# A two-layer gated cross-attention kernel: second attention with values centred in advance, gates placed by matmuls, and rows loaded straight from the parts

## The chip, the cores and the metric

One core of a Trainium2 chip. The metric is device time in microseconds (us) of one execution; the kernel before takes 1559.09 us (median of three runs, 1558.21 to 1559.24).

## The reference, cut to what matters

64 sequences of 128 tokens and width 256 go through two layers. Each layer adds tanh(gate) times an attention to x, then tanh(gate) times an FFN. The first attention is a differential softmax attention with 16 heads, the FFNs are quantised. The change is about the second attention, whose queries are the normed x, and whose keys and values are both the context:

```
gates: ig, fg = concat(q, k, v) @ kernel + bias     # 4 heads each
cs = cumsum(log_sigmoid(fg)); log_D = cs - cs.T + ig.T, causal
m = max(log_D); C = (q k / 8) * exp(log_D - m)
h = C / (max(|sum C|, exp(-m)) + 1e-6) @ v
out = (h - mean(h)) * rsqrt(var(h) + 1e-5) * outnorm   # per head of 64
```

As the mean of h over a head is C times the mean of v, the kernel centres the values over each head instead of h.

## The kernel before, in words

Five engines run five programs written out by hand (PE matmul, ACT, DVE, POOL, and SP, which only issues DMAs). All synchronise by semaphores; each engine, SP too, works its program strictly in its written order, so a wait holds up what stands behind it. x stays in SBUF throughout.

**First attention** (class Attention0, 0 to about 755 us). All engines follow one count of ticks, eight for a sequence. PE's order is maxima, weighted, transposes, scores. POOL's loop (L809 on) does for each b: finish (norm statistics, at some b), square(b-3), normed_queries(b+2), normalise(b-3) with a pow (L797). SP issues load_x (eight rows of x, 1 MB), load_context, stack_keys and max_rows. **First FFN** (Ffn0) follows, to about 1054 us.

**Second attention** (class Attention1) begins when the last x of the first FFN is there (`begin`). First, for 12 groups of four sequences: DVE normalises (`normalise`), PE transposes (`turn`, L1268), ACT copies to qt, PE makes the gates (`gates`, L1280), ACT copies them to g_row (L1377). After eight groups the gates of 32 sequences are moved from rows to one partition per head and sequence by DMAs (`spread`, L1194). DVE and ACT then take the log, two scans, and split results into three bf16 parts (L1498, L1501); DMAs write the parts to DRAM (`parts_out`, L1200), and for each pair p of sequences two DMAs bring them back as rows (`load_rows`, L1214 and L1215). The other 32 sequences' gates are made within the loop (late groups in iterations 0 to 7; spread at i = 8, parts_out at i = 12).

Loop over 32 pairs. In iteration i:

- PE: scores(i) (L1310), values(i) (context times a centring matrix, L1320), arg(i+1) (exponent's argument by matmuls of the rows, L1297 and L1298), weighted(i-1) (L1331, the numerator and the sum).
- ACT: copies the values (L1401), exp of arg(i+1) (L1394), copies the numerator (L1407), squares it (L1413), normalises x for the next FFN's maximum (L1420).
- DVE: combine(i) (L1507), add(i-5) (L1545), scale(i-4) (L1537), sum_squares(i-2) (L1513), at odd i normaliser (L1519 to L1530), norm statistics (L81), next_max (L1549).
- POOL: scaled(i-4) (a_hn, L1619), at odd i factor (pow, a_fac, L1614) and finish with its pow (L94 to L107).
- SP: keys(i+2), rows(i+2); the last FFN's weights at i = 18 (L1651, L1652).

SP's waits, which the prediction uses:

```
load_keys(p): wait v_pe >= p-2, s_pe >= p-2      # 2 DMAs, buffers: 3
load_rows(p): wait arg >= p-1                    # 2 DMAs from DRAM, buffers: 2
```

n_pe counts weighted, arg counts arg, s_pe counts scores. **Second FFN** (Ffn1) needs a maximum over all tokens, and starts when the second attention is done.

Of the kernel before, what the change touches and what calls it, by code (L numbers as in the profile page):

```python
# [15 lines left out]
P = 128  # L16
# [6 lines left out]
HD0 = D // NH0  # L23
NPAIR = NH0 // 2
# [18 lines left out]
class Shared:  # L43


    def __init__(self, nc, ctx, t):
# [36 lines left out]
    def finish(self, w, k, g):  # L83

        e, n, size = w.e, self.n[k], self.GROUP[k]
# [8 lines left out]
        e.tensor_tensor(apart, *two(1), ALU.subtract).then_inc(n["steps"], 1)  # L94
        e.tensor_tensor(total, *two(1), ALU.add).then_inc(n["steps"], 1)
        e.tensor_tensor(var, *two(2), ALU.add).then_inc(n["steps"], 1)
        w.wait_ge(n["steps"], 8 * g + 1)
        e.tensor_tensor(apart, apart, apart, ALU.mult).then_inc(n["steps"], 1)
        w.wait_ge(n["steps"], 8 * g + 3)
        e.tensor_scalar(self.neg_mean[:, rows], total, -0.5, 1.0, ALU.mult, ALU.mult).then_inc(n["steps"], 1)  # L100
        e.tensor_scalar(var, var, 1.0 / D, 1e-5, ALU.mult, ALU.add).then_inc(n["steps"], 1)
        w.wait_ge(n["steps"], 8 * g + 4)
        e.tensor_scalar(apart, apart, 0.5, 0.5, ALU.mult, ALU.mult).then_inc(n["steps"], 1)
        w.wait_ge(n["steps"], 8 * g + 7)
        e.tensor_tensor(var, var, apart, ALU.add).then_inc(n["steps"], 1)
        w.wait_ge(n["steps"], 8 * g + 8)
        e.tensor_tensor(self.rstd[:, rows], var, self.expo[:, 0:size], ALU.pow).then_inc(n["rstd"], 1)  # L107

    def wait_x(self, w, g):
        w.wait_ge(self.s_x[g % 4], 16 * (g // 4 + 1))  # L110
# [8 lines left out]
def build(nc, t):  # L119
    with ExitStack() as ctx:  # L120
# [48 lines left out]
        @block.gpsimd  # L169
        def _(e):  # L170
            w, s = Engine(e), sh.s
            e.memset(sh.ones[:, :], 1.0).then_inc(s["made"], 1)
            e.memset(sh.expo[:, :], -0.5).then_inc(s["made"], 1)
            ahead, rest = f0.pool(w)
            a0.pool(w, ahead)
            rest()
            a1.pool(w)
            f1.pool(w)
# [112 lines left out]
class Attention0:  # L291
# [10 lines left out]

    def __init__(self, sh, ctx, k_stack):
# [33 lines left out]

        self.ones_zeros = sh.x[0:2, 48:64, :].rearrange("p b d -> p (b d)")
# [3 lines left out]
            "st_pe", "exp", "o_pe", "o_sb", "b_pe", "div", "diff", "pool", "var", "n_t", "n_sb", "wo_pe", "x_new"))  # L342
# [21 lines left out]
    def sp(self, w, ahead):  # L364
        sh, s, e, t = self.sh, self.s, w.e, self.sh.t
        def load_x(g):
            rows = slice(8 * g, 8 * g + 8)
            if g == 6:
                w.wait_ge(s["one_rows"], 112)
            e.dma_start(sh.x[:, rows, :], t["x"][rows].rearrange("b p d -> p b d")).then_inc(sh.s_x[g % 4], 16)  # L370

# [31 lines left out]
        load_x(0)  # L403
# [6 lines left out]
        for tick in range(self.START, self.END):  # L410
            b, u = divmod(tick, 8)
            o, v = divmod(tick - 4, 8)
            if u == 4 and b % 8 == 2 and 0 <= b // 8 < 6:
                load_x(b // 8 + 2)
# [4 lines left out]
            if (tick + 12) % 16 == 0 and 0 <= (tick + 12) // 16 < NSEQ // 2:  # L419
                stack_keys((tick + 12) // 16, 1)  # L420
            if tick == -12:
                load_x(1)
# [347 lines left out]
    def pool(self, w, ahead):  # L770
# [6 lines left out]
        w.wait_ge(s["zeroed"], 4)  # L777
# [22 lines left out]

        for b in range(-3, NSEQ + 5):
# [8 lines left out]
            if 0 <= b - 3 < NSEQ:  # L810
                normalise(b - 3)
            ahead(b)
# [299 lines left out]
class Attention1:  # L1112
# [7 lines left out]
    WIDE, INIT = 96, 8  # L1120

    def __init__(self, sh, ctx, f0, fw):
# [16 lines left out]
        self.xn = sb("a1_xn", [P, 4, D])  # L1139
        self.expo = sb("a1_expo", [P, 4 * NH])  # L1140
        self.parts = sb("a1_parts", [P, 2, 3, P], BF16)
# [3 lines left out]
        self.v_aug = sb("a1_v", [P, 2, 2, NH * (HD + 1) + 32])  # L1145
        self.dec = sb("a1_dec", [P, 3, 2, 2, 2, P])
        self.num = sb("a1_num", [P, 8, NH, HD + 1])
# [5 lines left out]

        self.ind = self.xn_next[0:12, 0].rearrange("r i d -> r (i d)")
        self.s = sh.sems("a1_", (
            "load", "prep", "init", "xn", "qt_pe", "qt_sb", "g_pe", "g_sb", "scan", "log_f", "parts", "col_pe", "cols",
            "s_pe", "v_pe", "v_sb", "arg", "dec", "c", "n_pe", "n_sb", "sq", "ssq", "small", "fac", "hn", "scaled", "x_new",
            "minus", "xn_next", "next_max"))
        self.s_gctx = [sh.sem(f"a1_gctx{i}") for i in range(2)]
        self.s_spread = [sh.sem(f"a1_spread{i}") for i in range(2)]  # L1160
        self.s_out = [sh.sem(f"a1_out{i}") for i in range(2)]
# [3 lines left out]
    def begin(self, w):  # L1165
        w.wait_ge(self.f0.s["x_new"], NSEQ)

# [8 lines left out]
    def rows_landed(self, w, p):  # L1176
        w.wait_ge(self.s_row[p % 2], 32 * (p // 2 + 1))

    def sp(self, w):
        self.begin(w)  # L1180
        sh, s, e, t, NH, GRP = self.sh, self.s, w.e, self.sh.t, self.NH, self.GRP
# [7 lines left out]
        def spread(hf):  # L1189
            w.wait_ge(s["g_sb"], 8 * hf + 8)  # L1190
            for kind, dst in ((0, self.gi), (1, self.gf)):
                for n in range(NH):
                    row = 4 * kind + n
# [832 lines left out]
```

## Time and profile before

| | |
|---|---|
| median of three runs | 1559.09 us |
| profiled execution, its own time | 1564.45 us |
| its span, first to last instruction | 1562.7 us |
| PE busy | 1365.2 us (87%) |
| DVE busy | 1192.3 us (76%) |
| ACT busy | 1094.1 us (70%) |
| POOL busy | 633.9 us (41%) |
| mean granted TensorE clock | 0.941 of 2.4 GHz |

Busy shares are means over stages with different limits. The page's slices show PE nearly full up to about 1000 us and a dip between 1050 and 1130 us and again near 1330 to 1360 us; those two are the start and the end of the second attention.

### The profile page before, as it was taken

How to read it: one execution, taken by the hardware profiler on the slowest of the kernel's cores; microseconds unless marked ns; L12 is line 12 of the kernel's file. 1: busy time of each engine (PE TensorE's matmuls, PEld its weight loads, DVE VectorE, ACT ScalarE, POOL GpSimd, SP SyncE). 2: the span in 40 equal slices, each digit the busy share in tenths (PEclk: the TensorE clock that was granted, in tenths of full speed). 3: DMA queues.
4: the chain of work that ended last, by engine and by line, in shares of the span. 5: the costliest groups of instructions: out<-in, count | busy, mean ns of one | idle time of the engine just before them, and what ended most of it. 6: DMA issues, size and time to landing. Idle time of an engine off the chain costs nothing. (4 is left out here: it accounts for less than half of the span.)

```text
span 1562.7 us, 31126 instructions
## 1 busy us (share of the span) xinstructions
PE 1365.2 (87%) x11804; PEld 930.1 (60%) x11804; DVE 1192.3 (76%) x2022; ACT 1094.1 (70%) x1809; POOL 633.9 (41%) x971
## 2 busy tenths in 40 slices
PE   4899999999999999999789999975699988177686
PEld 2566666666666666666446666654477767133375
DVE  4478788878887788777779999853247999699785
ACT  2367777777777777777478888863346666499996
POOL 1044455546454544544744432312025767621000
PEclk9599999999999999999889999996699999599899
DMA  8655676566565755573100000004321310078299
GB/s 164 98 85 80 106 97 115 79 104 97 92 97 83 123 81 80 84 97 70 55 1 1 1 2 1 1 1 119 109 71 42 113 50 22 4 312 334 105 394 362
DMA packets 118488, 153.63 MB, mean 98 GB/s; under 512 B 13994, under 2 KB 86826, under 8 KB 112182
## 3 DMA queue, kind: packets, MB, share of 16 engines
q1 hardware_dynamic: 118052, 151.65, 43.0%
q8 instruction: 94, 1.54, 0.5%
q14 instruction: 54, 0.44, 0.1%
q10 hardware_dynamic: 288, 0.00, 0.0%
HBM read 65.82 MB, written 33.95 MB: 64 GB/s over the span
## 5 line engine op out<-in xcount | busy, mean ns | idle before, releaser
L694 DVE TENSOR_REDUCE neg_max<-psum 128x8 f32<-128x1024 f32 x256 | 313.3, 1224 | 75.6 <-PE psum L503 71.2
L631 ACT ACTIVATE exp_t<-psum 128x512 f32<-128x512 f32 x512 | 281.5, 597 | 48.2 <-PE psum L516 48.0
L797 POOL TENSOR_TENSOR rs<-rs,minus_half 128x16 f32<-128x16 f32 x64 | 186.8, 2918 | 5.0
L516 PEld LDWEIGHTS psum<-q_stack,k_stack 50*128 50x128 f32 x2048 | 136.8, 191 | 78.0 <-issue 75.5
L516 PE MATMUL psum<-q_stack,k_stack 50*128 50x128 f32 x2048 | 173.0, 289 | 0.8 <-ACT exp_t L631 0.7
L527 PE MATMUL psum<-exp_t,v_pad 128*32 128x256 f32 x2048 | 167.7, 400 | 0.0
L789 POOL TENSOR_TENSOR sq<-u 128x256 f32<-128x256 f32 x64 | 39.2, 612 | 302.1 <-DVE u L711 302.1
L636 ACT ACTIVATE o_t<-psum 128x512 f32<-128x512 f32 x128 | 76.5, 598 | 98.0 <-PE psum L527 97.7
L503 PE MATMUL psum<-k_stack,q_stack 48*128 48x256 f32 x1024 | 135.7, 344 | 7.4 <-DVE neg_max L694 6.0
L872 PE MATMUL psum<-f_w,f_xqt 128*128 128x512 bf16 x512 | 124.9, 386 | 4.6 <-DVE f_hid L1000 4.4
L503 PEld LDWEIGHTS psum<-k_stack,q_stack 48*128 48x128 f32 x1024 | 82.4, 192 | 56.5 <-issue 44.2
L620 ACT ACTIVATE q_stack<-psum 128x512 fp32r<-128x512 f32 x128 | 75.1, 587 | 49.0 <-PE psum L491 49.0
L81 DVE BATCH_NORM_STATS2 norm_stats<-x_state 128x6 f32<-128x256 f32 x256 | 102.9, 415 | 0.0
L1841 ACT ACTIVATE f_gelu<-psum,f_b,f_m 128x512 f32<-128x512 f32 x128 | 97.9, 1340 | 0.0
L1000 DVE SCALAR_TENSOR_TENSOR f_hid<-psum,f_sup,f_act 128x1024 f32<-128x1024 f32 x64 | 81.9, 1279 | 20.3 <-ACT f_act L937 19.6
L491 PE MATMUL psum<-ident,q_nat 128*128 128x128 f32 x512 | 85.6, 292 | 10.9 <-DVE q_nat L681 10.1
L544 PE MATMUL psum<-ident,o_t 128*128 128x128 f32 x512 | 86.0, 292 | 5.2 <-DVE x_state L721 5.2
L950 ACT ACTIVATE f_hqt<-psum 128x1024 bf16<-128x1024 f32 x64 | 65.5, 1023 | 32.5 <-PE psum L890 32.5
L1614 POOL TENSOR_TENSOR a_fac<-a_fac,a_expo 128x16 f32<-128x16 f32 x16 | 46.4, 2900 | 98.8 <-DVE a_fac L1530 98.8
L1802 PE MATMUL psum<-f_w_down,f_hq 128*128 128x256 bf16 x512 | 67.5, 280 | 20.4 <-DVE f_hq L1895 9.6
L1888 DVE TENSOR_REDUCE f_gmax<-f_gelu 128x1 f32<-128x1024 f32 x64 | 77.5, 1215 | 8.3 <-ACT f_gelu L1841 5.3
L491 PEld LDWEIGHTS psum<-ident,q_nat 128*128 128x128 f32 x512 | 60.2, 147 | 38.8 <-issue 25.9
(215 smaller groups left out, 3039.2 us busy)
## 6 DMA issues: line engine op xcount, KB each, us to landing
k_stack<-k_hi SPq DMA_DIRECT2D x256, 128.0 KB, 4.8
g_scratch<-f_gelu SPq DMA_DIRECT2D x24, 1024.0 KB, 4.0
f_gelu<-g_scratch SPq DMA_DIRECT2D x24, 1024.0 KB, 14.9
k_stack<-k_lo SPq DMA_DIRECT2D x128, 128.0 KB, 4.8
ctx_t<-in_ctx_t SPq DMA_DIRECT2D x64, 128.0 KB, 4.7
x_state<-in_x SPq DMA_DIRECT2D x8, 1024.0 KB, 7.7
a_ctx_g<-in_ctx_t SPq DMA_DIRECT2D x32, 256.0 KB, 3.2
a_kt<-in_ctx_t SPq DMA_DIRECT2D x64, 128.0 KB, 2.2
```

The costliest lines, as they stand in the source:

```text
L81: w.e.bn_stats(self.stats[:, k % 2, b % 16], self.x[:, b, :]).then_inc(n["moments"], 1)
L491: r = e.transpose(psum[:, 7, n * P:(n + 1) * P], self.q_nat[:, 2 * pair:2 * pair + 2, :].rearrange("p h c -> p (h c)"), ident[:, :])
L503: r = e.matmul(psum[:, j, o:o + D], self.q_st[rows, b % self.NQ, pair, :], self.k_st[rows, b // 2 % self.NK, pair // 2 % 2, pair % 2, :, p ...
L516: r = e.matmul(psum[:, 2 + j, o:o + P], self.k_st[rows, b // 2 % self.NK, pair // 2 % 2, pair % 2, i, pair // 4, b % 2, :], self.q_st[rows ...
L527: r = e.matmul(psum[32 * i:32 * i + 32, 5, (u % 2) * D:(u % 2) * D + D], self.v_pad[:, (b // 2) % 2, b % 2, 4 * u + i, :], self.prob[:, n ...
L544: r = e.transpose(psum[:, 4, n * P:(n + 1) * P], self.o_t[:, hf].rearrange("p u w t -> p (u w) t")[:, n, :], ident[:, :])
L631: e.activation(self.prob[:, n % 3, j].rearrange("p n w t -> p (n w t)"), psum[:, 2 + j, :], ACT.Exp).then_inc(s["exp"], 1)
L694: e.tensor_reduce(self.negm[:, b % 2, :, :, 2 * u:2 * u + 2].rearrange("p j w n -> p j n w"), psum[:, 0:2, :].rearrange("p j (n w k) -> p ...
L797: e.tensor_tensor(self.rs[:, i], self.rs[:, i], self.expo[:, :], ALU.pow).then_inc(s["pool"], 1)
L872: r = e.matmul(psum[:, bank + h, :], self.xqt[:, b % 2, c, :], weights[:, c, h * BANK:(h + 1) * BANK], start=c == 0, stop=c == 1)
L1000: e.scalar_tensor_tensor(out=self.hid[:, b % self.HS], in0=psum[:, 2:4, :].rearrange("p j c -> p (j c)"), scalar=self.s_up[:, b:b + 1], in ...
L1841: r = e.activation(self.gel[:, u % self.RING, j], psum[:, 2 * (u % 3) + j, :], ACT.Gelu, scale=self.m1[:, 3:4], bias=self.b1[:, ht:ht + 1])
```

## The change

1. **Values.** During the first attention SP loads each pair's context with tokens on partitions, POOL averages each head by halving adds and subtracts the mean (`centre`, eight instructions), and SP stores the result with a column of ones to DRAM (`v_scratch`). In the second attention PE's values and ACT's copy are gone; SP loads the pair's values (`load_values`), three buffers.
2. **Gates.** `place`: for each group two matmuls with a placing matrix put the gates where the spread put them, accumulating in PSUM bank 6; DVE copies the bank. g_row has two buffers. The spread is gone.
3. **Parts** stay in SBUF for each half; `load_rows` reads them from there with five DMAs. parts_out is gone.
4. **Normaliser.** ACT writes |sum| (L1407's place, `numerator`, two instructions), 1e-6 is added to exp(-m) once per half (`floor`), and three DVE instructions stay of five. scale is one instruction for both sequences.
5. **Order.** Gate weights and biases are loaded before `begin`, and DVE adds them up there. Groups overlap: gates(g-1), turn(g), place(g-1). log_forget(0) comes one group earlier on ACT, scan(0) at b = 41 instead of 43 on DVE; arg(0) comes before columns(0). ACT computes one Ln at its start.
6. **x** is loaded in the first attention in halves of four sequences, behind load_context. The counters of `finish` run through all stages (no other effect).

```diff
 Attention0.sp
-            if u == 4 and b % 8 == 2 and 0 <= b // 8 < 6:
-                load_x(b // 8 + 2)
...
+            if u == 7 and b % 8 in (2, 4) and 0 <= b // 8 < 6:
+                load_x(b // 8 + 2, b % 8 // 2 - 1)
+            if u == 5 and b % 2 == 0 and 0 <= b < NSEQ:
+                store_values(b // 2)
+            if u == 5 and b % 2 == 0 and 0 <= b + 2 < NSEQ:
+                load_values((b + 2) // 2)
 Attention0.pool
+        def centre(p):
+            n = self.CENTRED * p
+            v = self.v_in[:, :, :].rearrange("p b (n e) -> p (b n) e", e=HD1)
+            out = self.v_out[:, p % 2]
+            w.wait_ge(s["v_in"], 16 * (p + 1))
+            w.wait_ge(s["v_out"], 16 * (p - 1))
+            for i in range(6):
+                half = HD1 >> (i + 1)
...
+                w.wait_ge(s["centred"], n + i)
+                e.tensor_tensor(into, left, right, ALU.add).then_inc(s["centred"], 1)
...
+            e.tensor_scalar(self.v_mean[:, :], self.v_mean[:, :], 1.0 / HD1, 1.0, ALU.mult, ALU.mult).then_inc(s["centred"], 1)
...
+            e.tensor_tensor(out[:, :, 0:HD1], v, self.v_mean[:, :].unsqueeze(2).to_broadcast([P, 2 * NH1, HD1]),
+                            ALU.subtract).then_inc(s["centred"], 1)
...
             if 0 <= b - 3 < NSEQ:
                 normalise(b - 3)
+            if b % 2 and 0 <= b + 1 < NSEQ:
+                centre((b + 1) // 2)
 Attention1.sp
+        def load_values(p):
+            w.wait_ge(s["init"], self.INIT)
+            w.wait_ge(s["n_pe"], p - 2)
+            e.dma_start(self.v_aug[:, p % 3, 0:2 * NH * (HD + 1)], t["v_scratch"][p]).then_inc(self.s_v[p % 3], 16)
+
         def load_rows(p):
+            hf, row = p // 16, 8 * (p % 16)
             w.wait_ge(s["init"], self.INIT)
-            w.wait_ge(self.s_out[p // 16], 128)
+            w.wait_ge(s["parts"], 10 * hf + 10)
             w.wait_ge(s["arg"], p - 1)
-            e.dma_start(self.m_row[32:35, p % 2], t["am_scratch"][0, 2 * p:2 * p + 2].rearrange("b n c t -> c b n t")).then_inc(self.s_row[p % 2], 16)
-            e.dma_start(self.a_row[0:12, p % 2], t["am_scratch"][1, 2 * p:2 * p + 2].rearrange("b n c t -> (n c) b t")).then_inc(self.s_row[p % 2], 16)
+            for i in range(2):
+                e.dma_start(self.a_row[0:12, p % 2, i], self.parts[row + NH * i:row + NH * i + NH, hf, 1]).then_inc(self.s_row[p % 2], 16)
+            for c in range(3):
+                e.dma_start(self.m_row[32 + c:33 + c, p % 2], self.parts[row:row + 2 * NH, hf, 0, c]).then_inc(self.s_row[p % 2], 16)
...
         for i in range(self.NP):
             if self.late_group(i) is not None:
                 load_group(self.late_group(i))
-            if i == 8:
-                spread(1)
-            if i == 12:
-                parts_out(1)
+            if i + 3 < self.NP:
+                load_keys(i + 3)
             if i + 2 < self.NP:
-                load_keys(i + 2)
                 load_rows(i + 2)
+            if i + 3 < self.NP:
+                load_values(i + 3)
 Attention1.pe
+        def place(g):
+            hf, j = divmod(g, 8)
+            w.wait_ge(s["load"], self.ROWS)
+            w.wait_ge(s["g_sb"], g + 1)
+            if hf:
+                w.wait_ge(s["scan"], 1)
+            for kind in range(2):
+                o = (2 * hf + kind) * P
+                r = e.matmul(psum[:, 6, o:o + P], self.place[:, kind, 16 * (7 - j):16 * (7 - j) + P], self.g_row[:, g % 2, :],
+                             start=j == kind == 0, stop=j == 7 and kind == 1)
+            r.then_inc(s["placed"], 1)
...
             if i < self.NP:
                 scores(i)
-                values(i)
             if i + 1 < self.NP:
                 arg(i + 1)
             if 0 <= i - 1:
                 weighted(i - 1)
...
             if g is not None:
                 gates(g)
+                place(g)
 Attention1.dve normaliser(q)
-            w.wait_ge(s["n_sb"], 2 * q + 2)
-            e.scalar_tensor_tensor(out=d, in0=sums, scalar=-1.0, in1=sums, op0=ALU.mult, op1=ALU.max).then_inc(s["small"], 1)
-            w.wait_ge(s["cols"], q // 8 + 1)
-            e.tensor_tensor(d, d, self.exp_m[:, 4 * q:4 * q + 4], ALU.max).then_inc(s["small"], 1)
-            e.tensor_scalar(d, d, 1e-6, None, ALU.add).then_inc(s["small"], 1)
+            w.wait_ge(s["n_sb"], 4 * q + 4)
+            w.wait_ge(s["floor"], q // 8 + 1)
+            e.scalar_tensor_tensor(out=d, in0=d, scalar=1e-6, in1=self.exp_m[:, 4 * q:4 * q + 4], op0=ALU.add, op1=ALU.max).then_inc(s["small"], 1)
```

## Rows read from the trace of the kernel before

**Rows 1.** Busy us by stage: PE, weight load, DVE, ACT, POOL; PE clock, DMA, GB/s

```profile
100.00:700.00 600.00, 595.93 (x5964) 396.37 (x5963) 480.19 (x800) 443.33 (x886) 303.20 (x386) 1.00 0.62 94
...
1053.00:1122.00 69.00, 37.35 (x483) 28.61 (x481) 25.13 (x73) 22.64 (x42) 9.62 (x17) 0.65 0.39 109
...
1180.00:1316.00 136.00, 127.36 (x1060) 98.31 (x1059) 122.64 (x260) 88.88 (x139) 95.33 (x145) 0.99 0.22 64
```

**Rows 2.** Timeline of PE, one iteration: start us, us, instruction, [idle before]

```profile
1224.22 1.16 PE L1310 MATMUL psum<-a_qt,a_kt 64*128 64x128 f32 x16 [0.50 <-DVE a_dec L1507]
...
1226.31 0.38 PE L1297 MATMUL psum<-a_mask,a_ident 128*128 128x512 bf16 x1
...
1227.26 0.39 PE L1298 MATMUL psum<-a_m_row,a_a_row 35*128 35x512 bf16 x1
1227.58 2.02 PE L1331 MATMUL psum<-a_v,a_dec 128*128 128x96 f32 x16
```

**Rows 3.** Timeline of SP's queue beside it

```profile
1226.50 0.91 SPq L1207 DMA_DIRECT2D a_kt<-in_ctx_t  x2
1227.68 0.27 SPq L1214 DMA_DIRECT2D a_m_row<-am_scratch  x1
```

**Rows 4.** Timeline of PE, start of the second attention

```profile
1066.03 1.08 PE L1280 MATMUL psum<-a_qt,a_wgate 128*32 128x128 f32 x16 [9.70 <-DVE a_wgate L1464]
...
1103.47 1.08 PE L1280 MATMUL psum<-a_qt,a_wgate 128*32 128x128 f32 x16 [4.59 <-ACT a_qt L1370]
...
1122.42 0.61 PE L1297 MATMUL psum<-a_mask,a_ident 128*128 128x512 bf16 x1 [2.24 <-DMA a_a_row<-am_scratch]
```

**Rows 5.** Timeline of PE, weighted(0) and weighted(29)

```profile
1136.92 2.02 PE L1331 MATMUL psum<-a_v,a_dec 128*128 128x96 f32 x16
...
1314.58 2.02 PE L1331 MATMUL psum<-a_v,a_dec 128*128 128x96 f32 x16
```

**Rows 6.** Timeline of SP's queue: spread, parts_out, loads of a_row

```profile
1096.03 2.37 SPq L1194 DMA_DIRECT2D a_in_gate<-a_g_row  x4
...
1113.89 5.05 SPq L1200 DMA_DIRECT2D am_scratch<-a_parts  x8
...
1120.72 0.33 SPq L1215 DMA_DIRECT2D a_a_row<-am_scratch  x1
...
1189.40 0.31 SPq L1215 DMA_DIRECT2D a_a_row<-am_scratch  x1
```

**Rows 7.** Timeline of PE at i = 8, behind the second spread

```profile
1191.36 0.39 PE L1297 MATMUL psum<-a_mask,a_ident 128*128 128x512 bf16 x1 [1.35 <-DMA a_a_row<-am_scratch]
...
1192.64 3.01 PE L1331 MATMUL psum<-a_v,a_dec 128*128 128x96 f32 x16
```

**Rows 8.** Busy time by stage, columns as in rows 1

```profile
1103.00:1128.00 25.00, 15.70 (x141) 11.53 (x142) 8.05 (x26) 9.56 (x15) 0.00 (x0) 0.50 0.33 93
...
1194.00:1198.00 4.00, 4.00 (x30) 3.71 (x30) 1.37 (x5) 2.27 (x4) 3.83 (x8) 0.64 0.02 6
```

**Rows 9.** DMA issues: form, count, size, median us from issue to landing

```profile
f_w_down<-in_w_t SPq DMA_DIRECT2D x1, 1024.0 KB, 7.7
```

**Rows 10.** Costliest groups, 1000 to 1400 us: busy us, mean ns, idle before

```profile
L1619 POOL TENSOR_TENSOR a_hn<-a_hn,a_onorm 128x512 f32<-128x512 f32 x32 | 40.7, 1271 | 46.5 <-DVE a_hn L1537 46.5
...
L1519 DVE SCALAR_TENSOR_TENSOR a_den<-a_num 128x16 f32<-128x16 f32 x16 | 13.4, 836 | 0.0
...
L1522 DVE TENSOR_TENSOR a_den<-a_den,a_exp_m 128x16 f32<-128x16 f32 x16 | 2.8, 175 | 0.7
```

**Rows 11.** Timeline of POOL: first attention, and the last pow of a_fac

```profile
625.55 0.21 POOL L94 TENSOR_TENSOR norm_work<-norm_stats 128x8 f32<-128x8 f32 x1 [0.84 <-DVE norm_stats L81]
...
629.66 0.61 POOL L789 TENSOR_TENSOR sq<-u 128x256 f32<-128x256 f32 x1 [0.67 <-DVE u L711]
...
1337.76 2.90 POOL L1614 TENSOR_TENSOR a_fac<-a_fac,a_expo 128x16 f32<-128x16 f32 x1 [0.95 <-DVE a_fac L1530]
```

**Rows 12.** Waits of PE, 0 to 800 us: us in total, times, longest

```profile
PE psum L465 <- DMA ctx_t<-in_ctx_t: 8.7, 5, 4.7
```

More of the change, by code:

```diff
@@ L23 @@
 HD0 = D // NH0
+NH1 = 4
+HD1 = D // NH1
 NPAIR = NH0 // 2
@@ L1152, in __init__ @@
         self.xn_next = sb("a1_xn_next", [P, 2, 2, D])
+        self.place = self.xn_next[:, 1].rearrange("p i d -> p (i d)")[:, 0:15 * P // 4].rearrange("p (k c) -> p k c", k=2)
         self.ind = self.xn_next[0:12, 0].rearrange("r i d -> r (i d)")
         self.s = sh.sems("a1_", (
-            "load", "prep", "init", "xn", "qt_pe", "qt_sb", "g_pe", "g_sb", "scan", "log_f", "parts", "col_pe", "cols",
-            "s_pe", "v_pe", "v_sb", "arg", "dec", "c", "n_pe", "n_sb", "sq", "ssq", "small", "fac", "hn", "scaled", "x_new",
+            "load", "prep", "init", "xn", "qt_pe", "qt_sb", "g_pe", "g_sb", "placed", "scan", "log_f", "parts", "col_pe", "cols",
+            "floor", "s_pe", "arg", "dec", "c", "n_pe", "n_sb", "sq", "ssq", "small", "fac", "hn", "scaled", "x_new",
             "minus", "xn_next", "next_max"))
         self.s_gctx = [sh.sem(f"a1_gctx{i}") for i in range(2)]
-        self.s_spread = [sh.sem(f"a1_spread{i}") for i in range(2)]
-        self.s_out = [sh.sem(f"a1_out{i}") for i in range(2)]
+        self.s_v = [sh.sem(f"a1_v{i}") for i in range(3)]
         self.s_ctx = [sh.sem(f"a1_ctx{i}") for i in range(3)]
@@ L1421, in next_normed @@
             r.then_inc(s["xn_next"], 1)
-        for g in range(self.EARLY):
-            turned(g, 0)
-            turned(g, 1)
-            gates(g)
-            if g == 9:
+        for g in range(self.EARLY + 1):
+            if 0 <= g - 1:
+                gates(g - 1)
+            if g < self.EARLY:
+                turned(g, 0)
+                turned(g, 1)
+            if g == 8:
                 log_forget(0)
+        decay_exp(0)
         columns(0)
-        decay_exp(0)
         for i in range(self.NP + 12):
-            if i < self.NP:
-                values(i)
             if i + 1 < self.NP:
@@ L1990, in _one_rows, with _gate_rows @@
     return rows.reshape(2, -1)
+def _gate_rows():
+    rows = np.zeros((P, 2, 15 * P // 8), np.float32)
+    for kind in range(2):
+        for i in range(4):
+            for n in range(4):
+                rows[32 * i + 4 * kind + n, kind, 112 + 4 * i + n] = 1.0
+    return rows
 def kernel(**inputs):
```

290 lines of the change are left out of this document (152 added, 138 removed).

## The prediction

> **What bounds the kernel now.** The busy time by stage comes first [rows 1]. In the first attention (100 to 700 us) PE is busy 595.93 of 600 us, so there every microsecond that PE waits is lost for good. Between 1053 and 1122 us, the start of the second attention, PE is busy 37.35 of 69 us at a mean clock of 0.65: this stage is a row of waits. In the loop over pairs (1180 to 1316 us) PE has 127.36 and DVE 122.64 of 136 us, so two engines share the bound. The second view is PE's timeline of one iteration of that loop [rows 2]: iteration i issues scores(i), values(i), arg(i+1) and weighted(i-1). Scores take 1.1 us, arg starts at 1226.31 and weighted at 1227.58, so arg is 1.27 us, and weighted is about 1.95 us. The third is SP's timeline beside it [rows 3]: the keys are issued at 1226.50, when values end, the rows from 1227.68, when arg ends. Rows issued there are read by an arg almost two iterations later, and PE does not wait for them.
>
> The start is read from PE's timeline [rows 4]. It waited 9.70 us for the gate weights, and 4.59 us at 1098.8 while the gates of the first half were spread by DMA; the loop's first arg is at 1122.42. I call W(i) the end of weighted(i). W(0) is 1138.9, W(29) is 1316.6, so 29 iterations take 177.7 us, 6.13 each [rows 5].
>
> **What the change does, part by part.**
>
> *SP's order in the loop, which decides.* SP's iteration i now issues keys(i+3), rows(i+2), values(i+3). values(i+3) overwrites the buffer that weighted(i) reads and waits for n_pe of i+1, which is W(i). PE does weighted(i) in its iteration i+1. SP's next iteration, with keys(i+4) and rows(i+3), stands behind that wait. But arg(i+3) comes in PE's iteration i+2, right behind scores(i+2). So rows(i+3) cannot be issued before W(i), and PE has only scores to do until it needs them. Before, the same load had two iterations.
>
> How long is the chain from W(i) to the rows? SP wakes within 0.03 us (arg ends at 1227.65, the rows start at 1227.68 [rows 2, 3]). The values are one DMA from DRAM: 0.40, estimated from the keys, of which two take 0.91 [rows 3]; with gaps the values and the keys end at 1.44. Then the rows: five DMAs instead of two, and from SBUF. The nearest rows are the spread (4 in 2.37 us) and the parts' store (8 in 5.05), 0.59 and 0.63 each, against 0.31 for the old a_row load from DRAM [rows 6]. The two SBUF sources differ in shape and cost the same, so I take 0.64 with the gap: 3.2 us, and the last issue ends at W + 4.6. From the end of an issue to PE's start it was 1.65 us at i = 8 (1189.71 to 1191.36 [rows 6, 7]) and 1.4 at the first arg (1121.05 to 1122.42 [rows 4, 6]); I take 1.4. Rows are there at W + 6.0; bounds 4.3 (five issues of 0.31) and 6.3.
>
> Then comes arg(i+3) and weighted(i+1), whose end is the next W. At the full clock they take 1.27 + 1.95, a period of 9.2 us. But PE has then stood still for 4 to 5 us in each period. After the wait of 4.59 us the matmuls ran at the lower level, and from 1103 to 1128 the granted clock was 0.50, that is 1.2 GHz [rows 4, 8]; even the wait of 1.35 us was followed by a weighted of 3.01 us instead of 1.95 and a stretch at 0.64 [rows 7, 8]. At the lower level a matmul of arg took 0.61 us against 0.38 or 0.39 [rows 2, 4]; four of them, each overlapping the next by a tenth, are 2.2. I take 2.2 and 3.0: period 11.2 us. Scores, 1.1 or 2.2, are hidden behind SP, as are turn, gates and place of the late groups (some 4 us). 29 periods are 324.8. The late groups' own loads (0.95 each) stand in the chain three times: 2.9. The weights of the last FFN, 2 x 1 MB, are issued by SP at i = 18 just ahead of rows(21); the second landed after 7.7 us [rows 9] against 1.4 for rows, so once some 6 us. Together 334, less 177.7: **+156**.
>
> The Trainium skill ("TensorE: Matmul & The Clock Gate", section on how the oscillation bites in real kernels) says that a loop whose matmuls are shorter than its wait for a DMA falls back and starts cold in every tile. The trace agrees for one wait of 4.59 us. By the rule alone both groups would take double, 2.54 and 3.9, the period would be 12.4 and the whole 1739 us; the row with 3.01 speaks for a little less.
>
> *Values leave the loop.* values(i) on PE (1.0 us at full clock) and its copy on ACT (0.60) go. While SP sets the period this is worth nothing beyond W(0), below.
>
> *Packed normaliser.* Two of five small DVE instructions go, 0.21 us each with their gap, and the two halves of scale become one (0.07): 0.5 us per two iterations. The first of the remaining three still takes 0.84 us, as L1519 does against 0.175 for L1522 [rows 10], because its two inputs lie in SBUF too while POOL is in a_hn. With SP as the bound: nothing. Otherwise 11 pairs of iterations: -5.4. The Trainium skill ("GPSIMD Engine Reference", specification table) says that POOL shares its SBUF interfaces with DVE instructions of two SBUF inputs. By that a normaliser with a PSUM input would have saved 0.7 us more per pair.
>
> *The start.* Gate weights are loaded ahead: gates(0) goes at about 1057.5. The next constants are still waited for by DVE behind its fourth row: the last is issued near 1058.4 instead of 1061.9 and lands 3.75 us later, so the second group starts 3.9 us earlier, no more. Ten groups run as before; place (two matmuls, 0.3 to 0.55 us) goes into the wait that preceded gates. The spread and its 4.59 us go; the table loads now come one group earlier. DVE's scan then starts near 1096.7 instead of 1109.1, -12.4. Behind it remain turn(10,1), gates(10), turn(11), gates(11) and three places: 15 us at 1.2 GHz where there were 13.3. The store to DRAM and the reload go, but rows(0) lands during this anyway. Loop start: -11, and two values fewer before W(0): **-13** (bounds -8 and -20).
>
> *The end.* Loops on DVE and POOL no longer lag behind PE. The last pow of a_fac started 21.2 us after W(29) [rows 5, 11]; now it has to wait for W(29) + 3.0 (copy, square, sum), pow, finish and scaled (7.6), and then add, scale, sum and normaliser (2.9): 13.5. **-8**.
>
> *First attention.* POOL gets centre(p) once in two sequences. Halving adds: 0.61, 0.33, 0.23 and three of 0.2, a small multiply, and a subtraction over 512 elements that costs what a_hn costs, 1.27 [rows 10]; with gaps 3.8 us. It starts where POOL is free: at 624.7, until square at 629.66 [rows 11], so mostly it is hidden. But 14 times that gap also holds a finish (625.55 to 629.0). Then square is 2.3 us late, DVE's variance waits in front of find_max, and of this PE sees about 0.9: 14 x 0.9 = +12.6 (bounds 0 and 2.3 each). The eight-row load of x, which made PE wait 8.7 us in all for ctx_t, 4.7 of it at the very start [rows 12], is halved and put behind the context: -4.1. The values' load and store ahead of the context add 0.53 MB, 1.9 us, once at the start: +1.9. Later contexts have 3 us to spare. **+10** (bounds -4 and +32).
>
> **Sum.** +156 - 13 - 8 + 10 = +145 us, made on the profiled execution (1564.45 us, span 1562.7), which is 0.34% above the median of 1559.09. Added to the median: **1704 us**.
>
> **The rivals.**
> (B) The same wait, but PE keeps its clock. For it: from 1190 on it fell only for some 4 us and came back. Against: gaps now recur in every period. Period 9.2, loop +98, whole 1646 us.
> (C) The five row loads are cheap, 0.31 each, because they move 12 or 8 pieces only. For it: the old rows. Against: both SBUF sources. The period is 9.5 at the low clock, whole 1655 us; 7.5 at the full clock, 1597 us.
> (D) The other side: the rows are in time. That takes a chain from W to the rows no longer than scores, 1.1 us, or a W that SP does not wait for; it is decided by whether the wait for n_pe stands ahead of rows(i+3) in SP's order. I find no way around it in the code, and the wait of 1.35 us behind the spread at i = 8 shows that SP's order binds PE [rows 7]. Then: -13 at the start, -5.4 in the loop, -1 at the end, +10: 1550 us, and 1537 if the first attention comes out at its lower bound.
> (E) Centring holds the first attention up in every pair and not 14 times. At 2.3 us x 32, on top of the forecast: 1765 us.
>
> **The numbers.** Forecast 0.50; its own range is 1675 to 1735 (periods of 10.3 to 12.3). B 0.18, C 0.17, D 0.10, E 0.05. From 1597, where C at the full clock lies, to 1730 leaves out D, E and a rim of the forecast: 2 in 10. A change of under 0.2%, 3 us, could not be told from none. Faster is D, 0.09; the same 0.01; slower 0.90.
>
> **What would show it.** In the profile after: PE idle before L1297's matmul some 4 us in each iteration, released by the DMA of a_m_row from a_parts; five row DMAs per iteration on SP, near 0.6 us each, behind a wait for weighted; PE's clock at 0.5 to 0.7 between 1130 and 1450; DVE and ACT half idle there; no a_hn wait. Right in the parts: gates(0) near 1057, no wait before 1098, W(0) near 1126. Wrong: an iteration of 5.4 us, PE waiting for DVE, or rows issued ahead of weighted. The whole is wrong if the time falls under 1597.

## The result, and the profile after

The changed kernel takes 1720.06 us (median of four runs, 1717.09 to 1723.33), the kernel before 1559.16 us beside it: a ratio of 1.1029 (95% interval 1.1002 to 1.1056), 160.9 us slower. Ratios here and below are made from the runs within 1.5% of the fastest of their kernel, medians from all its runs. The profiled execution of after takes 1718.42 us with a span of 1716.6 us, against 1562.7 before.

Where the 153.9 us between the two spans are is found with four marks on PE's timeline: the start of the last down projection of the first FFN, W(0), W(29), and the end. The last down projection starts at 1052.10 before and at 1060.17 after; weighted(0) and weighted(29) of after stand in PE's timeline like this:

```profile
1124.07 2.02 PE L1385 MATMUL psum<-a_v,a_dec 128*128 128x96 f32 x16
...
1472.15 3.73 PE L1385 MATMUL psum<-a_v,a_dec 128*128 128x96 f32 x16
```

| stretch | before | after | difference | forecast |
|---|---|---|---|---|
| start to the last down projection of the first FFN | 1052.10 | 1060.17 | +8.1 | +10 |
| from there to W(0) | 86.8 | 65.9 | -20.9 | -13 |
| W(0) to W(29) | 177.7 | 349.8 | +172.1 | +156 |
| W(29) to the end | 246.1 | 240.7 | -5.4 | -8 |

The busy time of each engine by stage, with the columns of [rows 1]:

```profile
100.00:700.00 600.00, 588.10 (x5859) 389.42 (x5859) 472.11 (x790) 436.49 (x872) 391.75 (x592) 1.00 0.62 115
1060.00:1126.00 66.00, 45.79 (x605) 35.88 (x605) 29.06 (x79) 28.16 (x50) 8.42 (x15) 0.87 0.49 140
1180.00:1316.00 136.00, 94.39 (x455) 68.03 (x455) 58.14 (x116) 38.11 (x67) 45.65 (x74) 0.54 0.17 48
```

In the loop PE has 94.39 of 136 us where it had 127.36, at a granted clock of 0.54 instead of 0.99, and DVE has fallen from 122.64 to 58.14: no compute engine is the bound. A group on the page of after (columns: busy us, mean ns | idle before, releaser) names what is:

```profile
L1361 PE MATMUL psum<-a_mask,a_ident 128*128 128x512 bf16 x64 | 36.2, 565 | 108.3 <-DMA a_m_row<-a_parts 108.3
```

L1361 is the first matmul of arg: PE stands 108.3 us in front of it and waits for the rows. PE's timeline in after, one period (columns as in [rows 2]):

```profile
1299.88 0.61 PE L1361 MATMUL psum<-a_mask,a_ident 128*128 128x512 bf16 x1 [3.98 <-DMA a_m_row<-a_parts]
...
1302.03 3.73 PE L1385 MATMUL psum<-a_v,a_dec 128*128 128x96 f32 x16
1305.69 2.08 PE L1374 MATMUL psum<-a_qt,a_kt 64*128 64x128 f32 x16
1311.75 0.61 PE L1361 MATMUL psum<-a_mask,a_ident 128*128 128x512 bf16 x1 [3.98 <-DMA a_m_row<-a_parts]
```

The timeline of SP's queue beside it:

```profile
1305.79 0.34 SPq L1259 DMA_DIRECT2D a_v<-v_scratch  x1
1306.17 0.95 SPq L1253 DMA_DIRECT2D a_kt<-in_ctx_t  x2
1307.16 1.39 SPq L1267 DMA_DIRECT2D a_a_row<-a_parts  x2
1308.60 2.04 SPq L1269 DMA_DIRECT2D a_m_row<-a_parts  x3
```

Weighted gives way to scores at 1305.69; the values go out 0.10 us later, and behind them the keys and the five row loads, 0.68 us each. The last issue ends at 1310.64 and PE starts arg at 1311.75, 6.06 us behind weighted. From start to start arg takes 2.15 us and weighted 3.66, so the period is 11.87 us. PE's timeline at the start, against [rows 4]:

```profile
1065.78 1.08 PE L1331 MATMUL psum<-a_qt,a_wgate 128*32 128x128 f32 x16 [1.24 <-ACT a_qt L1430]
1075.11 1.97 PE L1319 MATMUL psum<-ident,a_xn 128*128 128x128 f32 x8 [7.39 <-DVE a_xn L122]
...
1083.61 0.64 PE L1331 MATMUL psum<-a_qt,a_wgate 128*32 128x128 f32 x16 [0.29 <-ACT a_qt L1430]
1086.46 0.65 PE L1331 MATMUL psum<-a_qt,a_wgate 128*32 128x128 f32 x16 [0.29 <-ACT a_qt L1430]
```

The 9.70 us wait for the gate weights is 1.24, and 7.39 us of it are back in front of the second group, where DVE stands at its constants. So the second group starts 1.9 us earlier against the last down projection than it did before (14.9 us behind it instead of 16.9). From the third group on the groups follow at 2.84 us with L1331 at 0.64 us, which is full clock; in the kernel before L1280 still took 1.08 us in the second, third and fourth group. The clock of the stage is 0.87 instead of 0.65 [rows 1].

### The profile page after: what moved, and what is told of

Its sections match the earlier page's. It is cut to its first block and busy times, and to the rows that moved or that the text cites. A ratio compares the mean times of both kernels' runs of the same rounds, so it can differ in the third digit from the quotient of the medians.

```text
span 1716.6 us, 31136 instructions
## 1 busy us (share of the span) xinstructions
PE 1424.8 (83%) x11612; PEld 966.5 (56%) x11612; DVE 1183.6 (69%) x1960; ACT 1079.2 (63%) x1811; POOL 738.7 (43%) x1228
## 5 line engine op out<-in xcount | busy, mean ns | idle before, releaser
L1571 DVE SCALAR_TENSOR_TENSOR a_dec<-psum,a_dec 128x1024 f32<-128x1024 f32 x32 | 39.2, 1225 | 219.6 <-PE psum L1374 219.6
L532 PE MATMUL psum<-k_stack,q_stack 48*128 48x256 f32 x1024 | 135.4, 343 | 13.5 <-DVE neg_max L723 13.2
L1453 ACT ACTIVATE a_dec<-psum 128x1024 f32<-128x1024 f32 x32 | 32.8, 1024 | 178.2 <-PE psum L1362 178.2
L1679 POOL TENSOR_TENSOR a_hn<-a_hn,a_onorm 128x512 f32<-128x512 f32 x32 | 40.4, 1262 | 220.6 <-DVE a_hn L1597 220.6
L1361 PE MATMUL psum<-a_mask,a_ident 128*128 128x512 bf16 x64 | 36.2, 565 | 108.3 <-DMA a_m_row<-a_parts 108.3
L1385 PE MATMUL psum<-a_v,a_dec 128*128 128x96 f32 x512 | 113.7, 413 | 0.8 <-ACT a_num L1462 0.8
L1385 PEld LDWEIGHTS psum<-a_v,a_dec 128*128 128x128 f32 x512 | 106.2, 316 | 13.6 <-issue 13.4
```

The costliest lines, as they stand in the source:

```text
L532: r = e.matmul(psum[:, j, o:o + D], self.q_st[rows, b % self.NQ, pair, :], self.k_st[rows, b // 2 % self.NK, pair // 2 % 2, pair % 2, :, p ...
L1385: r = e.matmul(psum[:, 4 + b, o:o + self.WIDE], self.dec[:, p % 3, j, b, h, :], self.v_aug[:, p % 3, v:v + self.WIDE], start=True, stop=True)
```

## The experiments

Single traces of the same code differ by up to 21 us by the last down projection of the first FFN (the last section has the rows), so what one profile shows is read from its stretches, W(0) to W(29) above all, and whole times only from medians.

**1. The order on SP (k1_values_later).** In SP's loop of the changed kernel:

```diff
-            if i + 3 < self.NP:
-                load_keys(i + 3)
             if i + 2 < self.NP:
                 load_rows(i + 2)
+            if 3 <= i + 1 < self.NP:
+                load_values(i + 1)
             if i + 3 < self.NP:
-                load_values(i + 3)
+                load_keys(i + 3)
```

> The changed kernel with SP's iteration i issuing rows(i+2), values(i+1), keys(i+3) instead of keys(i+3), rows(i+2), values(i+3): all five row loads stay, but no wait for weighted of the same or the following iteration stands ahead of them any more. Theory (the wait for W(i) in front of rows(i+3) makes the chain): PE's wait for the rows goes, DVE bounds the loop with about 5.9 us a period, W(0) to W(29) is about 172 us instead of 349.9, the granted clock is back above 0.9, whole 1541 us (1530 to 1555). Rival 1 (five loads from SBUF are too much for SP in themselves): SP's issues, 0.34 + 0.95 + 3.43 us, and its waits do not fit into PE's period, it stays at 6.5 to 8 us, whole 1565 to 1610. Rival 2 (the slow matmuls come from something else than PE's idle time): period over 8 us, whole over 1610.

Measured: 1560.96 us (median of ten runs), ratio to before 0.9998 (0.9966 to 1.0031). The loop takes 182.4 us, not 349.8, with all five loads from SBUF in it. Of PE's waits for the rows one of 4.0 us is left, behind the weights' loads (groups of k1, 1130 to 1310 us, columns as above):

```profile
L1361 PE MATMUL psum<-a_mask,a_ident 128*128 128x512 bf16 x58 | 25.0, 431 | 5.4 <-DMA a_m_row<-a_parts 4.0 <-ACT a_dec L1453 1.4
```

The wait in front of the rows is shown to be the cause. Both rivals fall by the whole time, but each left a mark. SP's queue needs 4.98 us a period, a little more than PE (4.3) and DVE (4.85); its timeline in k1, one period:

```profile
1264.30 0.44 SPq L1259 DMA_DIRECT2D a_v<-v_scratch  x1
1264.78 0.94 SPq L1253 DMA_DIRECT2D a_kt<-in_ctx_t  x2
1265.77 1.39 SPq L1267 DMA_DIRECT2D a_a_row<-a_parts  x2
1267.20 2.04 SPq L1269 DMA_DIRECT2D a_m_row<-a_parts  x3
1269.28 0.44 SPq L1259 DMA_DIRECT2D a_v<-v_scratch  x1
```

And the clock did not come back above 0.9 but to 0.76 (1190 to 1290 us). The median is 20 us over the 1541 expected. In the profiled run (1558.52 us) 10 of them are the loop (182.4 against 172), though two more traces of the same loop below take 174.8 and 172.6; 4.4 are the end, which is back at 245.2 us from 240.7 in after; 3 are ahead of W(0). So what after gained at its end came with its wait: behind a loop that PE does not stand in, it is gone. The runs of this version spread from 1547.68 to 1572.86 us.

**2. The chain's length (k2_rows_first).** The wait stays, the keys go behind the rows:

```diff
-            if i + 3 < self.NP:
-                load_keys(i + 3)
             if i + 2 < self.NP:
                 load_rows(i + 2)
+            if i + 3 < self.NP:
+                load_keys(i + 3)
             if i + 3 < self.NP:
                 load_values(i + 3)
```

> The changed kernel with one exchange: SP's iteration issues rows(i+2), then keys(i+3), then values(i+3). The wait for W(i) still stands ahead of rows(i+3), but the two loads of keys (0.97 us with their gap) no longer stand between. Theory (the period is the chain from W over SP's issues to the landing, then arg and weighted): rows are there at W + 5.1 instead of W + 6.1, the period falls from 11.87 to 10.9 us, the loop by 28 us, whole 1690 us. Rival (rows are late because of how long they take to land, not because of when they are issued, or PE's low clock holds the scores up as well): the period stays within 0.3 us of 11.87.

Measured, in one run: the steady period is 10.9 us, the loop 315.3 us (34.5 less, 28 expected). PE's wait fell from 3.98 us by as much as the keys' issues take, as its timeline in k2 shows:

```profile
1294.10 2.08 PE L1374 MATMUL psum<-a_qt,a_kt 64*128 64x128 f32 x16
1299.14 0.61 PE L1361 MATMUL psum<-a_mask,a_ident 128*128 128x512 bf16 x1 [2.96 <-DMA a_m_row<-a_parts]
```

So the period is the sum of SP's issues behind the wait, the landing, arg and weighted. The whole came to 1705.5 us and not 1690, as this run's first FFN ended 21 us later.

**3. The clock's share (k3_pe_fed).**

```diff
             if i < self.NP:
                 scores(i)
+            if 12 <= i < self.NP - 1:
+                for k in range(16):
+                    e.matmul(psum[:, 6, :], self.ident16[:, :], self.mask16[:, :, :].rearrange("p n t -> p (n t)"), start=True, stop=True)
```

> The changed kernel with 16 matmuls of 128x512 bf16 into a free PSUM bank behind scores(i) for i = 12 to 30; their results are not used. They fill PE's wait for the rows. Theory (the low clock follows from PE's wait and costs 2.7 us of the period: arg 2.15 against 1.27, weighted 3.73 against 1.95): in these iterations the granted clock is near 1.0, rows are still there at W + 6.1, the period is 9.3 us instead of 11.87, whole 1718 - 19 x 2.6 = 1669 us, although PE does more. Rival (matmuls are slow here for another reason, or the clock does not come back): the 16 matmuls take 6.9 us instead of 3.4, the period is 14.8 us, whole about 1774.

Measured, in one run: from i = 12 on the periods alternate between 9.3 to 10.0 and 10.5 to 11.0 us, the loop is 318.5 us, 31 less although PE does more, and the whole 1693.43 us. PE's timeline in k3:

```profile
1305.47 3.63 PE L1404 MATMUL psum<-a_mask,a_ident 128*128 128x512 bf16 x16
1310.45 0.39 PE L1361 MATMUL psum<-a_mask,a_ident 128*128 128x512 bf16 x1 [1.36 <-DMA a_m_row<-a_parts]
...
1311.73 3.49 PE L1385 MATMUL psum<-a_v,a_dec 128*128 128x96 f32 x16
1315.15 2.08 PE L1374 MATMUL psum<-a_qt,a_kt 64*128 64x128 f32 x16
1317.16 4.44 PE L1404 MATMUL psum<-a_mask,a_ident 128*128 128x512 bf16 x16
1321.44 0.38 PE L1361 MATMUL psum<-a_mask,a_ident 128*128 128x512 bf16 x1
```

The shortest periods are the 9.3 us of the theory. In every second one 1.36 us of idle time are left, and weighted and scores behind them still ran slow (3.49 and 2.08 us; granted clock 0.81 over 1320 to 1420 us). The low clock follows from the wait and is worth 1.1 to 2.6 us of each period. The size was forecast too high (19 x 2.6 = 49 us, measured 31): half of the periods stay slow, and the one behind the weights of the last FFN took 18.0 us, in after 16.4. The whole is 24 us over the 1669 expected, 8 of them ahead of W(0).

**4. The wait alone (k4_before_wait).** In the kernel before:

```diff
             if i + 2 < self.NP:
+                w.wait_ge(s["n_pe"], i)
                 load_keys(i + 2)
                 load_rows(i + 2)
```

> The kernel before with one wait more: SP waits for n_pe of i, that is for weighted(i-1), ahead of keys(i+2) and rows(i+2). That is the wait that the change puts ahead of the rows, without its five loads from SBUF. Theory (what costs is the wait times the length of the issues behind it): behind W stand keys 0.95, two row loads 0.65 and a landing of 1.4, so rows are there at W + 3.0, against scores and values of 2.1 us; the wait on PE is 0.9 us or less, the period at most 6.3 us, whole 1560 to 1585. Rival (the wait alone is enough to cost the time, since any recurring gap brings the clock down for the whole loop): period 7.5 us or more, whole over 1600.

Measured: 1587.63 us, ratio 1.0196 (1.0152 to 1.024). The loop takes 208.9 us against 177.7: 19 of the 29 periods are 6.3 to 6.8 us and ten 7.6 to 10.2. One of the short ones in PE's timeline of k4:

```profile
1271.76 0.39 PE L1298 MATMUL psum<-a_mask,a_ident 128*128 128x512 bf16 x1 [0.85 <-DMA a_a_row<-am_scratch]
```

The wait of 0.85 us is as expected, and the short periods keep to the theory up to 0.5 us; the ten long ones it did not foresee (late groups, and the clock at 0.90 over 1180 to 1316 us; five as long stand in the loop before too), and the whole is 3 us over its range. With experiment 1 there is a loop for each case: neither, 177.7 us; the wait alone, 208.9; five loads from SBUF alone, 182.4, and 174.8 and 172.6 in two more traces below with the same loop; both, 349.8. (The last two cases also lack values on PE, and SP loads the values in them, so the cases are not cleanly crossed; experiment 5 puts 1 us of other work a period back on PE from i = 12 on, and the loop takes 170.5.) The wait alone costs 31 of the 172 us, the loads alone 5 or nothing.

**5 to 7. Three single edits on the version of experiment 1.** More work for PE (k5_fixed_fed, three of the matmuls of k3 from i = 12 on):

> The version with SP's order rows(i+2), values(i+1), keys(i+3), and in it three matmuls of 128x512 bf16 into a free PSUM bank behind scores(i) from i = 12 on; their results are not used. Without them PE has 4.3 us of work a period, less than DVE (4.85) and SP (4.98), and its periods went 4.3, 4.3, 4.3, 5.7, 10.8. Theory (with values gone PE waits for DVE or the rows every few periods, its clock falls, and one period at 1.2 GHz costs more than values did): with 0.7 us more work, PE keeps 2.4 GHz, the periods from i = 12 to 29 are 5.0 to 5.3 with no 10.8 among them, the granted clock there is over 0.95, and W(12) to W(29) takes 90 us instead of 96. Rival (the long periods are waits for DVE's maximum of the last FFN's weights and for the landing of rows behind those weights, whatever the clock): the long ones stay, and W(12) to W(29) takes 96 us or more.

Measured: 1556.76 us in one run. No period of 10.8 us is left, and the granted clock in W(12) to W(29) is 1.00 instead of 0.86. Busy time in that stretch, columns as in [rows 1], first k5:

```profile
1218.00:1311.00 93.00, 85.75 (x667) 58.62 (x667) 86.51 (x152) 56.14 (x102) 71.34 (x106) 1.00 0.40 117
```

and k1:

```profile
1215.10:1311.60 96.50, 86.37 (x616) 63.82 (x616) 83.00 (x143) 56.15 (x102) 67.71 (x105) 0.86 0.39 112
```

But the stretch takes 93.2 us, against 96.5 in k1 and 94.2 and 93.4 in the traces of k6 and k7, which have no extra matmuls and a clock of 0.85 and 0.91 there. The theory was right about the clock and wrong about its worth: DVE is busy 86.5 of 93 us there, so a slower PE mostly uses up its slack. The constants (k6_fixed_constants):

```diff
-            if b == 3:
+            if b == 15:
                 constants()
```

> The version with SP's order rows(i+2), values(i+1), keys(i+3), and DVE's use of the mask, the norm's weights and the identity moved from behind row 3 to behind row 15 of the second attention's start. Theory (PE's 7.4 to 8.0 us wait there is DVE standing at those loads): the wait is under 1 us, gates(1) comes 7 us earlier relative to the end of the first FFN, and W(0) too, 62 us behind the end of the first FFN instead of 68. Rival (something else is late at the same time: the context of the next groups, or ACT): W(0) comes at most 2 us earlier.

Measured: 1553.17 us in one run. The wait of 7.4 to 8.0 us is gone, the first FFN's last down projection to W(0) is 59.4 us instead of 68.1; the theory held, with 2.6 us more than it expected. The centring (k7_fixed_centre_shift):

```diff
 Attention0.sp
-            if u == 5 and b % 2 == 0 and 0 <= b < NSEQ:
-                store_values(b // 2)
-            if u == 5 and b % 2 == 0 and 0 <= b + 2 < NSEQ:
-                load_values((b + 2) // 2)
+            if u == 7 and b % 2 and 1 <= b < NSEQ:
+                store_values((b - 1) // 2)
+            if u == 7 and b % 2 and 0 <= b + 1 < NSEQ:
+                load_values((b + 1) // 2)
 Attention0.pool
-            if b % 2 and 0 <= b + 1 < NSEQ:
-                centre((b + 1) // 2)
+            if b % 2 == 0 and 0 <= b < NSEQ:
+                centre(b // 2)
```

> The version with SP's order rows(i+2), values(i+1), keys(i+3), and POOL's centre one sequence later in the first attention: at the end of an even b, so not right in front of a finish, with the values' load and store on SP moved to u = 7 of an odd b. Theory (the change's cost in the first attention is 13 meetings of centre and finish, 0.85 us each, and one stand of POOL at centre(0), 6.7 us on PE against 4.7 before): both go, the first FFN ends at 1046 to 1050 us instead of 1061, whole about 1548 us. Rival (centring costs by taking part in every pair, by POOL's and DVE's shared access or the DMAs, wherever it stands): the first FFN ends at 1058 or later.

Measured: 1537.63 us, ratio 0.9864 (0.9805 to 0.9923); the last down projection starts at 1044.26. The busy time of k7 from 100 to 700 us, columns as in [rows 1]:

```profile
100.00:700.00 600.00, 600.00 (x6004) 398.97 (x6006) 483.44 (x808) 447.29 (x894) 398.66 (x605) 1.00 0.68 118
```

588.10 in after became 600.00 (before: 595.93, the rest being waits for a context [rows 12]): the meetings of centre and finish cost 11.9 us, and centring as such nothing there. In after, POOL's timeline at one meeting is this, and square is late at its end:

```profile
633.00 1.04 POOL L851 TENSOR_TENSOR v_out<-v_in,v_mean 128x512 f32<-128x512 f32 x1
...
635.96 1.65 POOL L113 TENSOR_TENSOR norm_rstd<-norm_work,norm_minus_half 128x8 f32<-128x8 f32 x1
637.57 0.61 POOL L819 TENSOR_TENSOR sq<-u 128x256 f32<-128x256 f32 x1
```

The second half of that theory fell: at the very start the second of the two waits for q_nat went, but a context is waited for in its place (waits of PE in k7, 0 to 100 us: us in total, times, longest; q_nat was 17.0 in after):

```profile
PE psum L520 <- DVE q_nat L710: 10.3, 1, 10.3
...
PE psum L494 <- DMA ctx_t<-in_ctx_t: 6.3, 1, 6.3
```

**8. All together (k8_all).**

> All four together: SP's order rows(i+2), values(i+1), keys(i+3); three matmuls into a free bank behind scores(i) from i = 12 on; DVE's constants behind row 15; centre one sequence later. By the theories of the three single edits: 1560 - 6 - 7 - 12 = 1535 us, ratio to the kernel before 0.985. If the gains do not add (the loop's clock and the start's depend on what came before): 1545 us, ratio 0.991.

Measured: 1526.6 us, ratio 0.979 (0.9745 to 0.9836), faster than both kernels. By the stretches of the first table: 1048.8, 59.5, 172.0 and 244.4 us.

**9 and 10. The normaliser (k9_den_first) and the values' queue (k10_values_on_act).** On top of k8:

```diff
         for i in range(self.NP + 12):
             if i < self.NP:
                 combine(i)
...
+            if i % 2 == 1 and 0 <= i - 2 < self.NP:
+                den((i - 3) // 2)
             if 0 <= i - 5 < self.NP:
                 add(i - 5)
```

(den is the first two instructions of normaliser), and for k10 also:

```diff
 Attention1.act
                 numerator(i - 1)
+                if 3 <= i + 2 < self.NP:
+                    e.dma_start(self.v_aug[:, (i + 2) % 3, 0:2 * NH * (HD + 1)], self.sh.t["v_scratch"][i + 2]).then_inc(self.s_v[(i + 2) % 3], 16)
```

> The version with all four edits (SP's order, matmuls into a free bank, constants behind row 15, centre one sequence later), and in it the first two instructions of the packed normaliser taken ahead of add and scale in DVE's iteration, so that POOL is not yet in a_hn when they run. Theory (the first one takes 0.86 us instead of 0.18 because its two inputs lie in SBUF while POOL works in a_hn): its mean falls to 0.2 us; DVE, which is busy 93 of 100 us in the loop, loses 0.34 us a period, and the loop W(0) to W(29) shortens from 172 us by 3 to 10 us (SP's 4.98 us a period is the next bound). Rival (the 0.86 us is the price of the instruction's form, a scalar and two inputs of 128x16, wherever it stands): its mean stays above 0.8 us and the time does not change.

> The same, and the values' load issued from ACT's queue behind numerator(i-1) instead of from SP's. Theory (SP's queue, 4.98 us a period with 0.34 us of it for the values, is the bound that is left once DVE is relieved): SP's period can fall to 4.6 us, the long run of 5.0 us periods goes to 4.9 (three extra matmuls keep PE at 5.0), the loop is up to 3 us shorter, the whole within 3 us of the version with SP's loads. Rival (an issue on ACT holds up exp of the argument, which PE waits for): the loop is 5 us or more longer.

Measured: k9 1525.0 us, ratio 0.9779 (0.9698 to 0.9859), loop 169.0 us; k10 1524.3 us, 0.9807 (0.9691 to 0.9922), loop 169.0. Neither can be told from k8: the loop's 3 us less (172.0 in k8) are about what two traces of one loop differ by (174.8 and 172.6 in k6 and k7), and taking the values' load off SP in k10 brought nothing beyond k9. The first instruction fell to 571 ns, not to 200, and the one left behind rose from 176 to 691 (groups of k9, 1130 to 1290 us):

```profile
L1596 DVE SCALAR_TENSOR_TENSOR a_fac<-a_den,a_ssq 128x16 f32<-128x16 f32 x14 | 9.7, 691 | 1.3
L1587 DVE SCALAR_TENSOR_TENSOR a_den<-a_den,a_exp_m 128x16 f32<-128x16 f32 x14 | 8.0, 571 | 0.0
```

The three instructions of the normaliser take 1.44 us together, in k8 they took 1.22, so DVE was not relieved. The rival falls too, since the price went over to another instruction of the same chain and does not belong to the form of the first; the timelines of DVE and POOL in the last section say what it is.

## Why the prediction was right

The forecast was 1704 us, in a range of 1597 to 1730; it is 1720.06. On the spans it is +153.9 us for +145: the loop came out 16.1 us over its forecast, and the start, 7.9 us below its own, hides half of that, which is luck.

**SP's order decides.** Right, and shown: taking the wait out of the rows' way gave back 167 of the 172 us (experiment 1). Its terms: rows at W + 6.0, measured 6.06, from issues of 0.68 us each instead of 0.64 and a landing of 1.1 instead of 1.4; arg 2.2, measured 2.15. **The mis-sized term is weighted**, taken as 3.0 from the one row behind a short wait [rows 7]; it took 3.66 in each steady period, since the clock did not come back within it. That is 29 x 0.66 = 19 us, more than the whole error of the loop (+156 forecast, +172.1 measured); two terms forecast too high hide the rest. The weights of the last FFN cost 4.5 us instead of 6, the late groups 0.9 instead of 2.9. The Trainium skill ("TensorE: Matmul & The Clock Gate", section on how the oscillation bites in real kernels) says that a loop whose matmuls are shorter than its wait for a DMA starts cold in every tile. The estimate by doubling, 3.9 us for weighted, is nearer to the trace's 3.66 than the 3.0 was, and by that rule the trace agrees; for arg, 2.54 by doubling, the trace has 2.15.

**The start.** Right in what happens: the gates of group 0 at 1065.78, 8 us behind the forecast's 1057.5 as the stage began 8 us later; the constants' wait stayed; no wait for a spread. That W(0) is at 1126.1 for "near 1126" is luck: the stage began 8 us later and was 8 us shorter. Its size was -20.9, just beyond the bound of -20. The step that failed is the clock. DVE's scan in after:

```profile
1101.05 0.29 DVE L1536 SCALAR_TENSOR_TENSOR a_scan<-a_gates,a_scan 128x128 f32<-128x128 f32 x1 [0.78 <-ACT a_scan L1442]
```

Against the last down projection it starts 16.1 us earlier than before (1109.1), not 12.4, although the second group came 1.9 us earlier and not 3.9: "ten groups run as before" did not hold, they came at full clock from the third on. Behind the scan the work was costed at 1.2 GHz; that stretch ran at 0.93, and W(0) came 25.0 us behind the scan's start instead of 29.8.

**The end.** -5.4 for -8. The last pow of a_fac started 17.0 us after W(29) (1475.88), not 13.5. The timelines of DVE and of POOL in after:

```profile
1477.77 1.23 DVE L1571 SCALAR_TENSOR_TENSOR a_dec<-psum,a_dec 128x1024 f32<-128x1024 f32 x1 [6.74 <-PE psum L1374]
...
1483.16 0.68 DVE L1603 TENSOR_TENSOR x_state<-x_state,a_hn 128x512 f32<-128x512 f32 x1
```

```profile
1482.07 2.90 POOL L1674 TENSOR_TENSOR a_fac<-a_fac,a_expo 128x16 f32<-128x16 f32 x1 [0.53 <-DVE a_fac L1590]
...
1492.83 2.90 POOL L1674 TENSOR_TENSOR a_fac<-a_fac,a_expo 128x16 f32<-128x16 f32 x1 [0.53 <-DVE a_fac L1590]
```

The mis-sized term is the 3.0 us from W(29) to the pow before it, which took 6.2: in DVE's order combine(30) stands ahead of the sum and the normaliser, and it waits for PE's scores(30), which run behind weighted(29). The other two terms, 7.6 and 2.9, measured 7.6 and 3.2.

**The first attention.** +8.1 for +10, but the two traces differ in the clock of their first 100 us (0.78 before, 1.00 after); k4, which is the kernel before up to there, ran them at 1.00 and has its mark at 1048.83, so beside that trace the cost is 11.3, with the spread of single traces on it. The 14 meetings at 0.9 us (12.6) were right: 11.9 us by experiment 7. The halved load of x removed the later waits for a context (4.0 us) but not the one at the start of [rows 12]: POOL stood 21 us at centre(0) for its values, and PE behind it, 6.69 us where the context had cost 4.7. That is 2.0 more, the size of the forecast's 1.9 (for which it gave no row), but by another way: PE stood for the queries behind POOL, not for the context. The timelines of POOL and of PE in after:

```profile
41.25 0.72 POOL L847 TENSOR_TENSOR v_out<-v_in 128x256 f32<-128x256 f32 x1 [20.96 <-DMA v_in<-in_ctx]
```

```profile
46.98 1.12 PE L520 MATMUL psum<-ident,q_nat 128*128 128x128 f32 x4 [6.69 <-DVE q_nat L710]
```

**The rivals.** B (clock stays) falls by the clock of 0.54 in the loop. C (cheap issues) falls by 0.68 us each. D (rows in time) is what experiment 1 made true, at 1561 us for its 1550. E (centring costs in each pair) falls by k7's 600.00 of 600.

## What to carry to other kernels

On a queue that issues in order, look at each wait together with everything that stands behind it: the wait alone cost 31 us here, the slow issues alone next to nothing, and both together 172. A load that overwrites a buffer late in use belongs behind the loads that are needed sooner; one exchange of three lines was worth 167 us. And where work is to be hidden on a side engine, put it where no other optional work meets it: the same centring cost 11.9 us in one place and nothing one sequence later.

## What the runs showed of the hardware

**A DVE instruction with two SBUF inputs waits for POOL's whole a_hn.** DVE's timeline in k9:

```profile
1216.06 1.08 DVE L1587 SCALAR_TENSOR_TENSOR a_den<-a_den,a_exp_m 128x16 f32<-128x16 f32 x1
1217.17 0.18 DVE L1589 TENSOR_TENSOR a_den<-a_den 128x16 f32<-128x16 f32 x1
...
1219.24 0.68 DVE L1596 SCALAR_TENSOR_TENSOR a_fac<-a_den,a_ssq 128x16 f32<-128x16 f32 x1
```

POOL's beside it:

```profile
1215.84 1.27 POOL L1687 TENSOR_TENSOR a_hn<-a_hn,a_onorm 128x512 f32<-128x512 f32 x1
1218.63 1.26 POOL L1687 TENSOR_TENSOR a_hn<-a_hn,a_onorm 128x512 f32<-128x512 f32 x1 [1.52 <-DVE a_hn L1603]
```

The same in k8, DVE's timeline and then POOL's:

```profile
1220.28 0.87 DVE L1587 SCALAR_TENSOR_TENSOR a_den<-a_den,a_exp_m 128x16 f32<-128x16 f32 x1
```

```profile
1219.85 1.27 POOL L1682 TENSOR_TENSOR a_hn<-a_hn,a_onorm 128x512 f32<-128x512 f32 x1 [1.41 <-DVE a_hn L1600]
```

POOL's instructions end at 1217.11, 1219.89 and 1221.12; the DVE instructions that overlap them end at 1217.14, 1219.92 and 1221.15, each 0.03 us later, whatever they would need themselves (0.18). Moving them changed which one pays. The prediction had the cause and thought of it as a slower instruction; it is a wait, and it shows as the length of the instruction that waits. The Trainium skill ("SBUF — State Buffer", section "SBUF: two separate sides") says that whichever of the two engines starts first has the shared pair of ports for its whole instruction; for a_hn this trace agrees. For POOL's pow it does not: in the rows of the end above, DVE's add, with two SBUF inputs too, starts 1.09 us into the pow of 2.90 us and takes its usual 0.68. Why the pow does not hold it up stays open; so the rule is shown here for a_hn alone.

**Issues from SBUF in small rows take SP 0.68 us each,** against 0.34 for the values' load from DRAM, which moves 260 KB: SP's time per issue does not go by bytes here. Whether source or shape sets it was not tried.

**The clock can be lower in a full stretch.** In k6 PE is busy 99 of 100 us and is granted 0.91, in the stretch before it, with the same work, 1.00 (columns as in [rows 1]):

```profile
500.00:600.00 100.00, 98.03 (x979) 65.11 (x975) 78.27 (x132) 72.80 (x146) 66.26 (x104) 1.00 0.67 120
600.00:700.00 100.00, 99.11 (x920) 65.12 (x917) 73.34 (x122) 67.81 (x136) 61.93 (x92) 0.91 0.57 104
```

Such dips, and the clock of 0.50 to 1.00 in the first 50 to 100 us, put the first FFN's last down projection anywhere from 1060 to 1081 us in six traces of code that is the same up to there. Their cause stays open.
